# Cross-attention with a top-10 row update: sums over lines and the row indices move from TensorE to VectorE's 32x32 transposes, and the key-bias products get narrower

## The reference

```
scores = x @ score_w + score_b                       # (8, 224)
topk_idx = top_k(scores, 10)                         # 10 rows of each batch
q = x[topk_idx] @ Wq.T + bq ;  k = ctx @ Wk.T + bk ;  v = ctx @ Wv.T + bv
attn = softmax(q k.T / sqrt(32))                     # per batch and head, over 750 lines
out = x ;  out[topk_idx] = (attn v) @ out_w.T + out_b
```

## Time and profile before

| | us |
|---|---|
| median of 3 runs (143.11 to 146.93) | 143.16 |
| the profiled execution's own time | 142.52 |
| its span | 140.7 |
| PE busy / PE weight loads busy | 134.0 / 127.1 |
| DVE busy | 80.4 |
| ACT busy | 25.9 |
| granted TensorE clock over the span (1 is full) | 0.993 |

### The profile page before, as it was taken

One profiled execution on the slowest core, in us unless ns is written; L12 is line 12 of the kernel. 1 busy time (PEld: TensorE's weight loads), 2 busy tenths in 40 slices (PEclk: granted clock), 3 DMA queues, 4 the chain that ended last, 5 costly groups with the idle time before them and its releaser, 6 DMA issues.

```text
span 140.7 us, 3072 instructions
## 1 busy us (share of the span) xinstructions
PE 134.0 (95%) x1312; PEld 127.1 (90%) x1312; DVE 80.4 (57%) x212; ACT 25.9 (18%) x57; POOL 6.1 (4%) x31
## 2 busy tenths in 40 slices
PE   4989999999999999999999999999999999999990
PEld 2567999899999989999999999999999999998970
DVE  1788545999951576288870674088128605754350
ACT  4122410030411240003140041005001400411110
POOL 7400000003000000000000000000000000000002
PEclk9999999999999999999999999999999999999997
DMA  4999999999996299899979976995880380000001
GB/s 138 417 417 418 408 413 399 439 423 433 412 359 286 42 383 399 295 397 410 426 288 290 321 318 188 323 319 219 269 298 11 57 356 38 0 0 5 0 5 49
DMA packets 6959, 37.52 MB, mean 267 GB/s; under 512 B 961, under 2 KB 961, under 8 KB 4642
## 3 DMA queue, kind: packets, MB, share of 16 engines
q1 hardware_dynamic: 6528, 37.00, 69.3%
q0 software_dynamic: 128, 0.33, 0.7%
q10 hardware_dynamic: 290, 0.01, 0.2%
HBM read 33.50 MB, written 3.83 MB: 265 GB/s over the span
## 4 chain that ended last, share of the span: by engine, by line
PE 72%; DMA 14%; SPq 7%; issue 2%; DVE 1%; POOLq 1%; POOL 0%; DVEq 0%
PE mix_ps L806 38%; PE logits_ps L787 23%; DMA ctx_r<-ctx_rows_dram 14%; PE logits_ps L773 5%; SPq L197 3%; SPq L204 3%; PE logits_ps L737 2%; PE logits_ps L703 1%; PE mix_ps L737 1%; POOLq L60 1%; DVE o_T L555 1%; PE misc_ps L821 1%; DVE heads L552 1%; PE misc_ps L755 0%; SPq L210 0%
## 5 line engine op out<-in xcount | busy, mean ns | idle before, releaser
L806 PE MATMUL mix_ps<-probs,ctx_r 125*128 125x160 f32 x384 | 54.3, 301 | 0.1
L806 PEld LDWEIGHTS mix_ps<-probs,ctx_r 125*128 125x128 f32 x384 | 52.6, 190 | 0.9 <-issue 0.5
L787 PE MATMUL logits_ps<-qk,ctx_c 128*125 128x160 f32 x240 | 33.4, 299 | 0.0
L787 PEld LDWEIGHTS logits_ps<-qk,ctx_c 128*125 128x125 f32 x240 | 32.9, 188 | 0.0
L503 DVE TENSOR_REDUCE col_max<-logits_ps 125x160 f32<-125x960 f32 x8 | 9.2, 1154 | 25.5 <-PE logits_ps L787 21.2
L773 PE MATMUL logits_ps<-qk,ctx_c 128*125 128x160 f32 x144 | 20.5, 302 | 0.1
L773 PEld LDWEIGHTS logits_ps<-qk,ctx_c 128*125 128x125 f32 x144 | 19.6, 188 | 0.8 <-issue 0.4
L356 ACT ACTIVATE mix<-mix_ps 128x320 f32<-128x320 f32 x16 | 7.0, 439 | 64.4 <-PE mix_ps L806 64.4
L541 DVE TENSOR_REDUCE prob_sum<-probs 125x160 f32<-125x960 f32 x8 | 14.7, 1846 | 4.0 <-ACT probs L352 4.0
L352 ACT ACTIVATE probs<-probs 125x480 f32<-125x480 f32 x16 | 9.3, 603 | 27.9 <-DVE probs L535 27.9
L404 DVE CUSTOM_DVE_ANT_0 product<-x_sb,score_w_sb 112x513 f32<-112x513 f32 x16 | 10.4, 690 | 4.1 <-DMA x_sb<-x_lines_dram 4.1
(11 more groups left out here) (121 smaller groups left out, 88.7 us busy)
## 6 DMA issues: line engine op xcount, KB each, us to landing
ctx_r<-ctx_rows_dram SPq DMA_DIRECT2D x8, 1536.0 KB, 7.6
ctx_c<-ctx_cols_dram SPq DMA_DIRECT2D x6, 1500.0 KB, 10.1
x_sb<-x_lines_dram SPq DMA_DIRECT2D x8, 520.0 KB, 9.4
out_dram<-x_sb SPq DMA_DIRECT2D x8, 448.0 KB, 12.4
ctx_c<-ctx_cols_dram SPq DMA_DIRECT2D x2, 750.0 KB, 14.5
ctx_c<-ctx_cols_dram SPq DMA_DIRECT2D x4, 375.0 KB, 15.5
wq_sb<-wq_dram SPq DMA_DIRECT2D x1, 1024.0 KB, 7.4
wk_sb<-wk_dram SPq DMA_DIRECT2D x1, 1024.0 KB, 9.9
```

The lines of the kernel that those rows point to most:

```text
L787: last = nc.tensor.matmul(logits_ps[n][0:S_P, t // BANK_T, (t % BANK_T) * HQ:(t % BANK_T + 1) * HQ], ctx_c[n][:, f, t, :], qk[:, b, f, :], ...
L806: last = nc.tensor.matmul(mix_ps[half][:, f * HQ:(f + 1) * HQ], ctx_r[n][0:S_P, t, c:c + P], probs[n][:, t, :], start=(t == 0), stop=(t == ...
```

## The change

- `sum_rows` and its semaphore go. `prob_sum` gets 128 lines, the last ones zeroed by GpSimd. `invert` works on VectorE alone: a transposing add over blocks of 32 x 32, three copies between quadrants, an add over the quadrants, a reciprocal of 5 columns a batch, a transpose that spreads the result over 32 lines, and four copies to `inv_sum`. It runs twice, for batches 0 to 6 after `sum_probs(6)` and for batch 7 after `sum_probs(7)`.
- `move_idx` leaves TensorE. The indices of batches 2 to 7 come from `idx_diag` (now 32 x 3 x 32) by a transposing add; those of batches 0 and 1 from `name_first`, seven small operations placed between `score(4)` and `score(5)`. `row_idx` is written in three pieces, ahead of `find_max(1)`; before, the copy came behind it.
- The key bias is masked (`key_heads`, 4 of 32 columns used) instead of the queries, so the product takes 20 and 60 columns instead of 80 and 240. `spread_key_dot` multiplies out of PSUM with `ident` on VectorE, for both groups; ScalarE's four copies for batches 0 and 1 (`copy_key_rows`) go. The transposing reduction is an add instead of a maximum, and for batches 0 and 1 it comes before `score(5)`.
- `project_values` no longer waits for the reciprocal, `project_queries(1)` no longer for the row indices.

```diff
@@ -266,13 +274,14 @@
                                    base=j, pattern=[[-1, 2], [-2, X_P]], channel_multiplier=2).then_inc(ties_done, 1)
...
             pool.memset(own_batch[:, :, :], 0.0).then_inc(consts_cleared, 1)
-            pool.memset(idx_diag[:, :], 0.0).then_inc(consts_cleared, 1)
+            pool.memset(idx_diag[:, :, :], 0.0).then_inc(consts_cleared, 1)
             pool.wait_ge(consts_cleared, 4)
...
                                base=0, pattern=[[-1, GB], [0, TOPK]], channel_multiplier=1).then_inc(own_done, 1)
-            pool.memset(idx_diag[0:1, TOPK:2 * TOPK], float(N)).then_inc(own_done, 1)
+            pool.memset(idx_diag[0:1, 0, TOPK:2 * TOPK], float(N)).then_inc(own_done, 1)
             pool.memset(regroup[:, :, :], 0.0).then_inc(regroup_done, 1)
             pool.memset(head_mask[:, :], 0.0).then_inc(mask_done, 1)
+            pool.memset(key_heads[:, :, :], 0.0).then_inc(heads_cleared, 1)
             for i in range(2 * FIRST):
...
@@ -281,8 +290,12 @@
             pool.wait_ge(mask_done, 1)
...
                 pool.memset(head_mask[h * DH:(h + 1) * DH, h:h + 1], 1.0).then_inc(mask_done, 1)
-
-            pool.wait_ge(idx_ready, 1)
+            pool.wait_ge(mask_done, 1 + HPT)
+            pool.memset(named[1][:, :], 0.0).then_inc(names_cleared, 1)
+            pool.wait_ge(names_cleared, 1)
+            pool.memset(prob_sum[P - QUAD:P, :, :], 0.0).then_inc(sums_cleared, 1)
+
+            pool.wait_ge(idx_ready, QUADS - 1)
             pool.indirect_dma_start(out=picked[:, :], out_offset=None, in_=x_rows,
...
@@ -337,14 +350,6 @@
                                          fold_ps[step][:, 0:HQ * FIRST].rearrange("p (e b c) -> p e b c", e=DT, b=FIRST),
...
 
-            def copy_key_rows():
...
             def exponential(b, n):
...
@@ -363,7 +368,6 @@
             copy_parts()
...
             copy_fold()
-            copy_key_rows()
             act.dma_start(out_b_sb[:, :], out_b).then_inc(out_b_in, 16)
...
@@ -435,7 +439,7 @@
 
...
                 nc.vector.scalar_tensor_tensor(
-                    out=idx_diag[0:nb, b0 * TOPK:b1 * TOPK].rearrange("p (b q) -> p b q", q=TOPK),
+                    out=idx_diag[0:nb, :, :].rearrange("p k c -> p (k c)")[:, b0 * TOPK:b1 * TOPK].rearrange("p (b q) -> p b q", q=TOPK),
                     in0=top_idx[0:nb, 0:TOPK].unsqueeze(1).broadcast_to([nb, nb, TOPK]),
...
@@ -451,9 +455,32 @@
                 dve.wait_ge(parts_ps_done, 2)
...
 
+            def name_first():
+                dve.wait_ge(names_cleared, 1)
+                cols = slice(0, FIRST * TOPK)
+                nc.vector.tensor_scalar(named[0][0:X_P, cols], one_hot[:, 0, cols], row_name[:, 0:1], None, ALU.mult)\
+                    .then_inc(name_step, 1)
+                dve.wait_ge(name_step, 1)
+                nc.vector.scalar_tensor_tensor(out=named[1][0:X_P, cols], in0=one_hot[:, 1, cols], scalar=row_name[:, 1:2],
+                                               in1=named[0][0:X_P, cols], op0=ALU.mult, op1=ALU.add).then_inc(name_step, 1)
+                dve.wait_ge(name_step, 2)
+                nc.vector.tensor_reduce(quad_named[:, 0:1], named[1][:, :].unsqueeze(1), AX.X, ALU.add, apply_transpose=True)\
+                    .then_inc(name_step, 1)
+                dve.wait_ge(name_step, 3)
+                for q in range(1, QUADS):
+                    nc.vector.tensor_copy(quad_named[0:QUAD, q:q + 1], quad_named[q * QUAD:(q + 1) * QUAD, 0:1]).then_inc(name_step, 1)
+                dve.wait_ge(name_step, 6)
+                nc.vector.tensor_reduce(first_idx[:, :], quad_named[0:QUAD, :], AX.X, ALU.add).then_inc(name_step, 1)
+
             def move_idx():
-                dve.wait_ge(idx_moved, 1)
-                nc.vector.tensor_copy(row_idx[:, :], row_idx_ps).then_inc(idx_ready, 1)
+                dve.wait_ge(idx_diag_done, 1)
+                nc.vector.tensor_reduce(idx_cols[:, :], idx_diag[:, :, :], AX.X, ALU.add, apply_transpose=True).then_inc(idx_summed, 1)
+                dve.wait_ge(idx_summed, 1)
+                dve.wait_ge(name_step, 7)
+                nc.vector.tensor_tensor(row_idx[0:QUAD, :], idx_cols[:, 0:1], first_idx[:, :], ALU.add).then_inc(idx_ready, 1)
+                for k in range(1, QUADS - 1):
+                    m = min(QUAD, BQ - k * QUAD)
+                    nc.vector.tensor_copy(row_idx[k * QUAD:k * QUAD + m, :], idx_cols[0:m, k:k + 1]).then_inc(idx_ready, 1)
 
...
@@ -480,20 +507,23 @@
                         pair_ps[step % 2][1][:, 0:HQ // 2 * (b1 - b0)].rearrange("p (e b c) -> p e b c", e=DT, b=b1 - b0))\
...
 
-            def copy_key_dot(g):
...
+            def spread_key_dot(g):
                 b0, b1 = GROUPS[g]
-                if g:
-                    dve.wait_ge(key_dot_ps, 2)
-                    for e in range(DT):
-                        nc.vector.tensor_copy(
-                            key_rows[:, b0:b1, e, :],
-                            key_ps[g][e * QUAD:(e + 1) * QUAD, 0:HC * (b1 - b0)].rearrange("p (b c) -> p b c", b=b1 - b0))\
-                            .then_inc(key_rows_done, 1)
+                nb = b1 - b0
+                dve.wait_ge(ident_done, 1)
+                dve.wait_ge(key_dot_ps, g + 1)
+                for e in range(DT):
+                    lines = slice(e * QUAD, (e + 1) * QUAD)
+                    nc.vector.tensor_tensor(
+                        key_rows[:, b0:b1, e, :].rearrange("p b (h q) -> p b h q", h=HPT),
+                        key_ps[g][lines, 0:nb * TOPK].rearrange("p (b q) -> p b q", b=nb).unsqueeze(2).broadcast_to([QUAD, nb, HPT, TOPK]),
+                        ident[lines, e * QUAD:e * QUAD + HPT].unsqueeze(1).unsqueeze(3).broadcast_to([QUAD, nb, HPT, TOPK]), ALU.mult)\
+                        .then_inc(key_rows_done, 1)
                 dve.wait_ge(key_rows_done, DT * (g + 1))
...
                     key_rows[:, b0:b1, :, :].rearrange("p b e c -> p (b e c)").rearrange("p (k c) -> p k c", c=QUAD),
-                    AX.X, ALU.max, apply_transpose=True).then_inc(key_dot_done, 1)
+                    AX.X, ALU.add, apply_transpose=True).then_inc(key_dot_done, 1)
 
...
@@ -537,16 +567,41 @@
                         shift[0:S_P, :].unsqueeze(1).broadcast_to([S_P, BANK_T, HQ]), ALU.add).then_inc(shifted, 1)
...
             def sum_probs(b, n):
+                dve.wait_ge(sums_cleared, 1)
                 dve.wait_ge(exp_done, 2 * b + 2)
-                nc.vector.tensor_reduce(prob_sum[:, b, :], probs[n][:, :, :].rearrange("p t c -> p c t"), AX.X, ALU.add)\
+                nc.vector.tensor_reduce(prob_sum[0:S_P, b, :], probs[n][:, :, :].rearrange("p t c -> p c t"), AX.X, ALU.add)\
                     .then_inc(sum_done, 1)
 
-            def invert():
...
+            def invert(part, b0, b1):
+                at = 7 * part
+                bs = slice(b0, b1)
+                dve.wait_ge(key_dot_done, 2)
+                dve.wait_ge(sum_done, b1)
+                nc.vector.tensor_reduce(
+                    quad_sum[:, 0, bs, :].rearrange("p b k -> p (b k)"),
+                    prob_sum[:, bs, :].rearrange("p b c -> p (b c)").rearrange("p (k c) -> p k c", c=QUAD),
+                    AX.X, ALU.add, apply_transpose=True).then_inc(inv_step, 1)
+                dve.wait_ge(inv_step, at + 1)
+                for q in range(1, QUADS):
+                    nc.vector.tensor_copy(quad_sum[0:QUAD, q, bs, :], quad_sum[q * QUAD:(q + 1) * QUAD, 0, bs, :])\
+                        .then_inc(inv_step, 1)
+                dve.wait_ge(inv_step, at + 4)
+                nc.vector.tensor_reduce(all_sum[:, bs, :], quad_sum[0:QUAD, :, bs, :].rearrange("p q b k -> p b k q"), AX.X, ALU.add)\
+                    .then_inc(inv_step, 1)
+                dve.wait_ge(inv_step, at + 5)
+                nc.vector.reciprocal(inv_all[:, bs, :], all_sum[:, bs, :]).then_inc(inv_step, 1)
+                dve.wait_ge(inv_step, at + 6)
+                nc.vector.transpose(inv_rows[:, bs, :].rearrange("p b c -> p (b c)").rearrange("p (k c) -> p k c", c=QUAD),
+                                    inv_all[:, bs, :].rearrange("p b k -> p (b k)").unsqueeze(2)
+                                    .broadcast_to([QUAD, (b1 - b0) * CB, QUAD])).then_inc(inv_step, 1)
+                dve.wait_ge(inv_step, at + 7)
+                for h in range(HPT):
+                    nc.vector.tensor_copy(
+                        inv_sum[h * DH:(h + 1) * DH, :, :].rearrange("p e (b q) -> p e b q", b=B)[:, :, bs, :],
+                        inv_rows[:, bs, :].rearrange("p b (e h q) -> p h e b q", e=DT, h=HPT)[:, h]).then_inc(inv_done, 1)
 
             def finish_heads():
-                dve.wait_ge(inv_done, 1)
+                dve.wait_ge(inv_done, 2 * HPT)
                 for e in range(DT):
...
@@ -585,13 +640,15 @@
             copy_parts()
...
             dve.wait_ge(bias_in, 16)
-            nc.vector.tensor_copy(key_rep[:, :, :], bias_sb[:, 1, :].unsqueeze(2).broadcast_to([P, DT, QUAD]))\
```

(41 more changed lines are left out.)

38 lines of the change are left out of this document (11 added, 27 removed).

## The result

The changed kernel takes 0.988 of the time of the kernel before (95% interval 0.9854 to 0.9905), about 1.7 us of 143.1. A second set of runs gave 0.9891 (0.9833 to 0.9948). The forecast was 142.1 us, 0.8% less, in a range of 141.2 to 143.4 us; 0.988 of the 143.16 us of before is 141.4 us. The median of all six runs is 142.57 us beside 143.13, but three of the six, and two of the six of before, ran 1.5% or more above the fastest of their kernel, and the ratios leave such executions out. The profiled execution took 141.29 us with a span of 139.5; the time is 1.23 us under that of the profiled execution of before.

What follows compares the result with a forecast made beforehand. The prediction took the transfer of batch 0's context rows, then TensorE's queue, to bound the kernel. Its terms, 0 + 0.29 + 0.87 - 0.1 = 1.06, say 1.1 us, gave 143.16 - 1.1 = 142.1 us, range 141.2 to 143.4.

Steps and rivals of the forecast that it cites:

- rival (a): Row indices before `weigh(1)` give their gain too, needing a VectorE shift of 0.3 us: 141.4 us, chance 0.13.
- What bounds it: Whole kernel: transfer of batch 0's context rows until 31.04 us, then TensorE alone from `weigh(0)` to the value projection.
- Part 1, the row indices: Before `weigh(1)`: TensorE freed of 0.62 us, VectorE's `find_max(1)` 0.9 us later, a stall of 0.6 us.
- five operations in series: VectorE's index work ahead of `find_max(1)`: the count held against a shift of only 0.3 us.
- net 0: At `weigh(1)`: the 0.6 us stall swallows the 0.62 us freed; bounds a gain of 0.2, a loss of 0.4.
- The gather and the early operations: Gather lands half a microsecond before its transposes; `name_first` and `spread_key_dot(0)` fit VectorE's idle time before `score(5)`: cost nothing.
- Part 2: Key-bias products of batches 2 to 7 on TensorE: 60 columns instead of 240, saving 0.29 us.
- Part 3: `sum_rows` leaves TensorE at `weigh(7)`, saving 0.87 us; VectorE's block for batches 0 to 6 takes 5.96 us.
- a stall of `weigh(7)`: If adds cost 1.77 ns an element, VectorE's block takes 6.85 us, stalling 0.25; 0.1 put in, range 0 to 0.3.
- The sum: Whole kernel: 0 + 0.29 + 0.87 - 0.1 = 1.06 us gained, say 1.1.

Runs made afterwards that it cites:

- experiments 4: Changed kernel with two, then all three, row-index writes on ScalarE (the latter also adding batches 0 and 1 into `idx_diag` early): ratios to before 0.9887 and 0.9868.
- experiment 5: Changed kernel with five more small copies on VectorE behind the row-index work, ahead of `find_max(1)`: one time, 143.06 us.
- experiment 3: Changed kernel with the row indices back on TensorE and without `name_first`, run twice: ratios to the kernel before 0.9914 and 0.9909.
- index_back2: Second run of the changed kernel with the row indices back on TensorE and without `name_first`: ratio to the kernel before 0.9909.
- experiment 7: Changed kernel with the seven small operations of `name_first` behind `score(6)` instead of ahead of `score(5)`: ratio to the kernel before 0.9989.
- experiment 8: Changed kernel with a maximum in place of the add in `sum_probs`, same shapes and strides: single time 144.97 us, with late loads.

## Why the prediction was right, and where its sizes were off

The mechanism was right; the gain came out larger than forecast, 1.7 us by the ratio against 1.1. That puts the time at 141.4 us, which is the time of rival (a). It wasn't rival (a) all the same: it needed a shift of 0.3 us on VectorE, and the shift is 0.94 with a stall in front of `weigh(1)`.

- **What bounds it** held: before `weigh(0)` the transfer, after it TensorE's queue.
- **Part 1, the row indices.** VectorE's shift was forecast at 0.9 us and is 0.94. (The prediction's "five operations in series" counts the index product in; four stand in the trace behind it.) That the wait for the exponential takes back part of the 0.62 us held, and experiments 4 and 5 show that wait move with VectorE's work both ways. The stall in front of `weigh(1)` was forecast at about 0.6 us and is 0.33 in this profile, as `weigh(0)` began 0.23 later. The term "net 0" was mis-sized, or rather it isn't one number: it is a gain of 0.26 us where the context rows land late against `find_max(0)`, and a loss of 0.2 where nothing waits for them. In the changed kernel `weigh(1)` starts at the later of two times: TensorE's, `weigh(0)` + 6.52, and VectorE's, `find_max(0)` + 14.43. With `move_idx` it is TensorE's with 0.62 more, so long as that needn't wait for the index product (experiment 3). With the starts of before (31.07, 23.88) this gives 38.21 for the kernel before and 38.31 for the changed one, a loss of 0.1. With those of the changed profile (31.30, 23.54, and the 0.19 of the table) it gives 38.44 and 38.16, a gain of 0.28. I took both engines' times from one execution, and the difference of the two starts, which the loads set, decides the sign: it is 7.19 us in the profile of before, 7.55 in `index_back2` and 7.76 in the changed profile, and by these sums gain and loss part at 14.43 - 7.14 = 7.29. The bounds given were a gain of 0.2 and a loss of 0.4; the gain just passes the better one. In the pair of profiles `weigh(1)` moved by only 0.04 to 0.07 us, near the forecast of 0, but that is luck: the changed execution's `weigh(0)` happened to begin 0.23 later.
- **The gather and the early operations** cost nothing that a distance shows, as said; experiment 7 gives the price without cover.
- **Part 2**: 0.29 forecast, 0.30 measured.
- **Part 3**: 0.87 forecast, 0.87 measured, with and without the other parts. The block for batches 0 to 6 was forecast at 5.96 us and took 5.45 (111.80 to 117.25): the four copies took 1.28 and not 1.8. So the 0.1 us set aside for a stall of `weigh(7)` isn't there. The row I leaned on for it, `sum_probs`, was a wrong neighbour: not the add makes it slow (experiment 8), and the large operations of the block, which read in order, go at the fast rate. Its one strided add did take more than the slope gives, 0.38 us for 0.30.
- **The sum**: 1.06 forecast. The pair of profiles gives 1.23; the ratio of the runs gives 1.7 (1.4 to 2.1), the second set 1.6 (0.7 to 2.4). 0.87 + 0.30 + 0.26 = 1.43 is what the parts give when the context rows land as late against `find_max(0)` as in `index_back2` and the changed profile. The rest, up to 0.3, is not explained. What is known is that the profiled execution of before, 142.52 us, was shorter than all six runs of its kernel (142.58 and more), so the pair of profiles may understate the gain.

The changes of the whole time inside 0.3 us (experiments 3 and 4) are argued from distances in profiles and are not settled by times.

## What to carry to other kernels

Before moving small work off the engine that sets the pace, look up what that engine waits for next and what stands ahead of that on the engine that gets the work: 0.62 us came off TensorE here and at most 0.26 arrived, because four small operations of 0.94 us went in front of the one exponential it needed. The same writes on ScalarE, idle there, cost nothing that the profile shows. And when single executions start differently, measure from an event behind the disturbance to the event in question, and keep in mind that a wait between two chains has a different price depending on which of them came late.

## What the runs showed of the hardware that was not expected

VectorE's forms in the changed kernel: count | busy us, mean ns | idle us.
```profile
L533 DVE TENSOR_REDUCE col_max<-logits_ps 125x160 f32<-125x960 f32 x8 | 9.3, 1157 | 18.8 <-PE logits_ps L827 15.2 <-PE logits_ps L813 3.5
...
L580 DVE TRANSPOSE_TENSOR_REDUCE quad_sum<-prob_sum 128x35 f32<-128x1120 f32 x1 | 1.3, 1346 | 0.1
...
L599 DVE COPY inv_sum<-key_rows 32x280 f32<-32x280 f32 x4 | 1.2, 298 | 0.1
...
L599 DVE COPY inv_sum<-key_rows 32x40 f32<-32x40 f32 x4 | 0.7, 175 | 0.1
...
L589 DVE TENSOR_REDUCE all_sum<-quad_sum 32x35 f32<-32x140 f32 x1 | 0.4, 381 | 0.0
...
L589 DVE TENSOR_REDUCE all_sum<-quad_sum 32x5 f32<-32x20 f32 x1 | 0.2, 173 | 0.0
```
The transposing add of 1120 elements takes 1346 ns, on the slope of the transposing maximum, and the key bias's transposing reduction of 960 elements takes 1166 ns as an add where it took 1167 as a maximum: the add costs no more than the maximum. `sum_probs`, 960 elements in 1846 ns as an add and 1834 as a maximum, reads its six terms 160 elements apart in SBUF, while `find_max` reads six terms, each three of them 160 apart, out of PSUM in 1154 to 1157. The add over the quadrants reads four terms 40 apart in SBUF: from 20 to 140 elements it grows by 381 - 173 ns, that is 1.73 ns an element. So these strided reductions of four and six terms from SBUF are slow and the one from PSUM isn't. Whether the stride or the shortness of the groups does it is not told apart: all reductions in order in these traces are transposing ones over 32 terms. The Trainium skill, VectorE: DVE Perf Modes, section on the perf-mode tier table, gives `tensor_reduce` in float32 one element a cycle; the traces agree for the transposing reductions, which read in order, at 1.04 ns an element (345 ns at 160 elements, 1346 at 1120). `find_max` out of PSUM, of which there is one size only, doesn't speak against it; the two strided reductions from SBUF do. The same table gives a float32 copy within SBUF twice that rate, and here the trace agrees: (298 - 175) / 240 = 0.51 ns an element, against 1.04 for the reductions.

Small VectorE operations follow each other at 0.17 to 0.19 us when each moves to another quadrant of partitions, though the elements are one or five: five copies of one column took 0.84 us in experiment 5.
